# Making part of the gathered far keys by one-hot products in the second attention's main loop

## The chip, the cores and the metric

The kernel runs on one core of one Trainium2 chip, as one program. The metric is the time of one execution on the device in microseconds (us). Each kernel is run several times and the median counts.

## The reference

The model has two layers on 2048 tokens of 128 features: an attention and a mixture of experts each, all with a layer norm in front and a residual behind. The change lies in the second layer's attention. It picks keys for each query:

```
c_kv = x @ W_dkv
s_i = relu(einsum('bthd,bsd->bths', x @ idx_wq, x @ idx_wk))   # 4 index heads
I = einsum('bths,h->bts', s_i, idx_w)
I = where(local, inf, I)       # the last 64 keys are always taken
I = where(causal, -inf, I)
_, idx = top_k(I, 96)          # so 32 far keys by index score
key_c, value = (c_kv @ W_uk)[idx], (c_kv @ W_uv)[idx]
key_r = pope((x @ W_kr)[idx], angles_k)    # angle by the key's rank
attn = softmax((q_c . key_c + q_r . key_r) * scale)   # 8 heads
out = (attn . value) @ W_out
```

The kernel multiplies W_uk into the queries and W_uv into the output, so that a key is one row of 64 numbers: 32 of c_kv, 32 of the softplus of x @ W_kr, which is then turned by an angle that depends on its rank. The 32 far keys of a query are 32 such rows, and they differ from query to query.

## The kernel before, in words

The tokens are cut into 16 tiles of 128 queries. `projections1` computes the key rows, the queries and the index products' operands, keeps the rows in `rows` [128, 16, 64] and writes them to a table in DRAM, `key_table`. It also ranks the first three tiles and issues the first 40 gathers.

`selected_attention` is the main loop. All its engines walk through one list of work, written out ahead by `selected_schedule`, in **slots**: 8 slots for each tile, one group of 16 queries in each. Each engine takes its own items of the list in that order and waits by semaphores; nothing is reordered when it runs. A slot holds, where they exist:

- ("score", t, g), TensorE: the masked scores of a group into one of three banks: mask (L1874), the 256 nearest keys (L1876), the far keys (L1882).
- ("q", ...), ("far", ...), ("p", ...), TensorE, emptied by ScalarE: transposes of queries (L1848), of far keys (L1852) and of probabilities (L1855) through two banks `a1_turn` that all of them share in turn. ("y", ...) is the output product (L1858), which VectorE adds to x (L1821).
- ("max", ...), ("exp", ...), ("den", ...), ("norm", ...): the softmax, on VectorE and ScalarE.
- ("ctx", t, c), TensorE: the weighted sum of half a tile (L1894, L1899); it is the last reader of the far keys.
- ("idx", ...), ("relu", ...), ("sum", ...), ("rank", ...): index scores of a tile some slots ahead on TensorE (L1933, L1934), ScalarE and VectorE (L1786), and its ranking on VectorE in 13 steps (max, max_index, match_replace four times over: L1720, L1723, L1726). `index_schedule` spreads them evenly by their widths over slots 0 to 106. They end with the transpose of the 32 places into `placeT` (L1733).
- ("keys", t, half), VectorE: the rotation of 16 gathered columns of far keys in place (L1092 to L1098), two slots ahead of their use, that of tile t's first half at slot 8t and of its second at slot 8t + 4. ("spin", ...) is the same for queries.

POOL has only the gathers (L1622): one indirect DMA fetches one column, that is one far key row for each of 128 partitions. A tile has 32 columns (tile 0: 16). Partition 32b + r of column i holds the key of rank r of query 32b + i. They go into a ring of four buffers `far`, so tile t waits for the context sums of tile t - 4:

```
if t >= RING:
    pool.wait_ge(ctx_full, 2 * (t - RING + 1))
```

SP's queue issues the few other DMAs of the loop: a copy of half of qT for each tile, the second mask, and the angles for the queries' rotation.

Of the kernel before, what the change touches and what calls it, by code (L numbers as in the profile page):

```python
# [1100 lines left out]
def projections1(nc, dram, x, ident, keep):  # L1101
    with ExitStack() as ctx:
# [22 lines left out]
        flipped = sb("first_flipped", [P, FAR], U32)  # L1125
        work = norm_work(sb, "2")
# [13 lines left out]
        loads = [(keep["idx_w"], "idx_w"), (keep["cap0"], "cap0"), (keep["cap"], "cap"), (cos_k, "cos_k"), (sin_k, "sin_k"),  # L1140
# [40 lines left out]
        with nc.Block() as block:  # L1181
# [85 lines left out]
            def _(dve):  # L1267
# [38 lines left out]
                def first_rank(t):  # L1306
# [4 lines left out]
                    last, cap = (values, keep["cap0"]) if t == 0 else (values[:, index_width(t) - P:], keep["cap"])  # L1311
# [125 lines left out]
PLACES = 6  # L1437
# [34 lines left out]
def selected_schedule(slot, ranking):  # L1472
# [13 lines left out]
    work += [("far", t, j % NG // 2)] if j % 2 == 0 and 0 <= t < NT else []  # L1486
    work += group("max", j - 2) + group("exp", j - 3)
# [9 lines left out]
    work += [("ahead", part, 0)] if 0 <= part < 3 + AHEAD else []  # L1497
    ahead = j + 2
# [30 lines left out]
def gather_list():  # L1529

    return [(t, i) for t in range(NT) for i in range(gathers(t))]


def landed(t, half):

    return 256 * (t // RING + (0 if t % RING == 0 and half else 1))
# [12 lines left out]
def selected_attention(nc, dram, x, ident, keep):  # L1549


    with ExitStack() as ctx:
# [15 lines left out]
        probsT = sb("a1_probsT", [P, 3, NG, P], F32)  # L1568
        biggest = sb("biggest", [P, NG], F32)
# [9 lines left out]
        mask_in, y_added, q_copied = (sem(n) for n in ("mask_in", "y_added", "q_copied"))  # L1579
        sums_done = lambda n: n - (n + NIDX - 1) // NIDX  # L1580
# [4 lines left out]
        TURNS = ("q", "far", "p", "y")  # L1585
# [4 lines left out]
        rotations = [w for w in schedule if w[0] in ("keys", "spin")]  # L1590

        with nc.Block() as block:
            @block.sync
            def _(sp):
# [5 lines left out]

                for t in range(NT):
# [25 lines left out]
            def _(act):  # L1627
                def empty_turn(kind, t, i):
# [32 lines left out]
                for kind, t, i in schedule:  # L1661
                    if kind in TURNS and kind != "y":
# [42 lines left out]
            def _(dve):  # L1705
                own = Order(dve, own_sem)

                def rank(t, i):
# [4 lines left out]
                    if i == 0:  # L1713
                        dve.wait_ge(summed, sums_done(idx_no["idx", t, len(index_chunks(t)) * NIDX - 1]))

                        cols, cap = (slice(0, w), keep["cap0"]) if t == 0 else (slice(w - P, w), keep["cap"])
# [110 lines left out]
            def _(pe):  # L1827
                def fill_turn(kind, t, i):
# [5 lines left out]
                    elif before:  # L1834
                        pe.wait_ge(turn_free, free_no[before])
# [451 lines left out]
```

## Time and profile before

| | us |
|---|---|
| median of 3 runs | 2267.05 |
| fastest and slowest of them | 2263.79, 2666.24 |
| the profiled execution | 2263.79 |
| its span, first to last instruction | 2263.8 |

The page covers the whole program. The first attention takes its first two thirds, the first experts follow, and the second attention begins near 1500 us; its main loop runs from about 1580 to 2217 us, and the last experts end the program. An engine's busy share over the whole span says little about the loop, so the loop is read by stretches. In the stretches a mean granted clock (PEclk) of 1.00 is 2.4 GHz and 0.50 is 1.2 GHz. Slots are found in the timeline by VectorE's rotations of far keys: the first is tile 0's, and each further tile has two.

### The profile page before, as it was taken

Reading aid. Unit: us, or ns where it says so; the run is one execution under the profiler, and the core shown is the slowest. Engines: PE = TensorE matmul, PEld = TensorE weight load, DVE = VectorE, ACT = ScalarE, POOL = GpSimd, SP = SyncE. Lnnn points to the kernel's source line nnn. Section 1 sums busy time; section 2 is a strip of 40 time slices with the busy share of each in tenths; the row PEclk is TensorE's granted clock in tenths of the full one; section 3 lists DMA queues with packets and bytes.
Section 4 is the critical chain, followed back from the end, with each engine's and each line's share of the span. In section 5 each row is a group of like instructions: output and inputs, shape, how many; then the busy total and the mean of one; then the engine's idle time right before and its main releaser. Section 6 shows DMA issues by size and latency. Waiting matters only on the chain. (4 is left out here: it accounts for less than half of the span.)

```text
span 2263.8 us, 56900 instructions
## 1 busy us (share of the span) xinstructions
PE 2100.6 (93%) x22674; PEld 1263.2 (56%) x22674; DVE 1789.1 (79%) x3457; ACT 1732.0 (77%) x3507; POOL 1828.5 (81%) x1239
## 2 busy tenths in 40 slices
PE   5899999999999999999999989986999899988878
PEld 1466666666666666666666646652454444444444
DVE  7788888888888888888888658978868986887214
ACT  5798898998989988988989945657566775775543
POOL 4899999999999999999999945627777777777720
PEclk9999999999999999999999989978579996999878
DMA  4000000000000000000000000111211111111101
GB/s 153 1 2 2 2 2 2 2 2 2 2 2 2 2 2 2 2 2 2 2 2 2 2 15 23 39 39 27 52 38 32 38 33 38 31 38 36 39 10 37
DMA packets 44688, 43.19 MB, mean 19 GB/s; under 512 B 21312, under 2 KB 33424, under 8 KB 44176
## 3 DMA queue, kind: packets, MB, share of 16 engines
q1 hardware_dynamic: 28560, 23.35, 3.6%
q0 software_dynamic: 15872, 16.28, 3.1%
q8 instruction: 178, 2.92, 0.5%
q14 instruction: 78, 0.64, 0.1%
HBM read 33.83 MB, written 1.57 MB: 16 GB/s over the span
## 5 line engine op out<-in xcount | busy, mean ns | idle before, releaser
L380 POOL TENSOR_TENSOR probs_lo<-probs,probs_hi 128x1024 f16<-128x1024 f32 x512 | 1076.7, 2129 | 43.0 <-ACT probs L430 42.6
L494 DVE TENSOR_REDUCE part_max<-aux 128x1 f32<-128x512 f32 x1024 | 677.9, 687 | 91.0 <-PE aux L568 86.7
L429 ACT ACTIVATE probs_hi<-scores 128x512 f16<-128x512 f32 x1024 | 630.2, 615 | 134.6 <-PE scores L601 117.3
L430 ACT ACTIVATE probs<-scores 128x512 f32<-128x512 f32 x1024 | 636.6, 622 | 0.0
L1622 POOL DMA_INDIRECT far<-key_table,placeT x456 | 451.9, 991 | 142.9 <-issue 138.7
L617 PE MATMUL acc<-v,probs_hi 128*128 128x65 f16 x4096 | 451.1, 193 | 2.3 <-POOL probs_lo L380 2.3
L619 PE MATMUL acc<-v,probs_hi 128*128 128x64 f16 x4096 | 452.3, 195 | 0.0
L621 PE MATMUL acc<-v,probs_lo 128*128 128x65 f16 x4096 | 450.6, 192 | 0.0
L617 PEld LDWEIGHTS acc<-v,probs_hi 128*128 128x128 f16 x4096 | 382.5, 96 | 82.6 <-POOL probs_lo L380 2.5
L619 PEld LDWEIGHTS acc<-v,probs_hi 128*128 128x128 f16 x4096 | 380.0, 97 | 75.5
L568 PE MATMUL aux<-k_a,q_a 128*128 128x512 f16 x1024 | 392.1, 383 | 5.2 <-DVE roped L480 2.1
L600 PE MATMUL scores<-q_a,k_a 128*128 128x512 f16 x1024 | 388.9, 380 | 6.6 <-ACT probs L430 6.5
L601 PE MATMUL scores<-q_b,k_b 65*128 65x512 f16 x1024 | 390.0, 381 | 0.0
L621 PEld LDWEIGHTS acc<-v,probs_lo 128*128 128x128 f16 x4096 | 381.6, 99 | 0.0
L601 PEld LDWEIGHTS scores<-q_b,k_b 65*128 65x128 f16 x1024 | 100.1, 98 | 112.6 <-issue 0.5
L568 PEld LDWEIGHTS aux<-k_a,q_a 128*128 128x128 f16 x1024 | 100.1, 98 | 83.1 <-DVE part_max L494 13.8
L600 PEld LDWEIGHTS scores<-q_a,k_a 128*128 128x128 f16 x1024 | 100.4, 98 | 81.5 <-ACT probs L430 26.0
L851 POOL TENSOR_TENSOR e_hid_lo<-e_hid,e_hid_hi 128x512 f16<-128x512 f32 x64 | 74.3, 1162 | 61.3 <-ACT e_hid_hi L803 61.3
L472 DVE TENSOR_TENSOR rope_term<-aux,cos 128x512 f32<-128x512 f32 x128 | 88.5, 691 | 26.4 <-PE aux L551 23.4
L1786 DVE SCALAR_TENSOR_TENSOR space<-space,idx_w 128x512 f32<-128x512 f32 (+4 forms) x111 | 72.8, 656 | 44.0 <-ACT space L1675 40.7
L1876 PE MATMUL a_score<-near_keys,qT 64*128 64x256 f32 x256 | 103.6, 489 | 0.0
L480 DVE TENSOR_TENSOR roped<-aux,rope_term 128x512 f32<-128x512 f32 x128 | 88.6, 692 | 17.6 <-DVE aux L475 1.0
(329 smaller groups left out, 3935.5 us busy)
## 6 DMA issues: line engine op xcount, KB each, us to landing
far<-key_table,placeT POOLq DMA_INDIRECT x496, 2.4
qT<-qT SPq DMA_DIRECT2D x16, 256.0 KB, 2.9
e_w<-in_e_w SPq DMA_DIRECT2D x48, 64.0 KB, 1.9
x<-in_x SPq DMA_DIRECT2D x4, 256.0 KB, 3.9
cos<-in_cos SPq DMA_DIRECT2D x1, 1024.0 KB, 6.8
sin<-in_sin SPq DMA_DIRECT2D x1, 1024.0 KB, 8.9
e_w<-in_e_w SPq DMA_DIRECT2D x2, 512.0 KB, 3.9
out<-x SPq DMA_DIRECT2D x4, 256.0 KB, 2.7
```

Source lines behind the costliest of these rows:

```text
L380: pool.tensor_tensor(probs_lo[:, slot], probs[:, wide], probs_hi[:, slot], ALU.subtract).then_inc(low_ready, 1)
L429: act.activation(probs_hi[:, slot, i], bank, ACT.Exp, scale=float(DH0) ** -0.5)
L430: act.activation(probs[:, wide, i], bank, ACT.Exp, scale=float(DH0) ** -0.5).then_inc(probs_ready, 1)
L494: dve.tensor_reduce(part_max[g % 2][:, n % QT, n // QT:n // QT + 1], bank, AX.X, ALU.max).then_inc(aux_free, 1)
L568: ins = pe.matmul(bank, qa[g % QRING][:, t * P:(t + 1) * P], ka[h % 2][:, c * CH:(c + 1) * CH], start=True, stop=True)
L600: pe.matmul(out, ka[h % 2][:, keys], qa[g % QRING][:], start=True, stop=False)
L601: pe.matmul(out, kb[h % 2][:, keys], qb[g % QRING][:], start=False, stop=True).then_inc(scores_ready, 1)
L617: pe.matmul(out, probs_hi[:, n % SLOTS, i, queries], high, start=(kt == 0 and t == 0), stop=False, skip_group_check=True)
L619: pe.matmul(out[:, 0:DH0], probs_hi[:, n % SLOTS, i, queries], low, start=False, stop=False, skip_group_check=True)
L621: ins = pe.matmul(out, probs_lo[:, n % SLOTS, i, queries], high, start=False, stop=(kt == KT0 - 1), skip_group_check=True)
L1622: pool.indirect_dma_start(far[m][:, i, :], None, keep["table"], bass.IndirectOffsetOnAxis(ap=placeT[t % PLACES][:, i:i + 1], axis=0)).then ...
L1876: pe.matmul(b[:, 0:WIN], qT[t % 2][0:KW, 0, 4 * g:4 * g + 4].rearrange("k i a h -> k (i a h)"), near[:, t * P:t * P + WIN], start=False, s ...
```

## The change

In tiles 3 to 9 (`MADE`) POOL gathers only columns 0 to 15. Columns 16 to 31 are made by TensorE from `rows`, which is in SBUF: the product of a one-hot matrix (which key each partition wants) and the rows of all keys up to the tile's end.

- After the ranking of such a tile VectorE also casts the places to half precision (`place16`). SP stores the part that belongs to columns 16 to 31 to DRAM (four DMAs) and loads all 2048 places of it back to all 128 partitions (one DMA, 512 KB, `placeB`), in `spread_places`.
- ("hot", t, k), k = 0 to 3, VectorE: for each of the t + 1 key tiles one comparison of 512 places with the partition's key number, which gives the one-hot tiles of four columns. They are written into `qi`, over index queries that are no longer needed: a ring of 4 tiles for t = 3, of 8 after it. A place in the ring is written again when TensorE has read it.
- ("make", t, k), one slot later, TensorE: (t + 1) x 2 x 4 products of 128x128 with 64 columns into a turn bank; the rows are split into a high and a low half-precision part (`split`), so that their sum is close to the float value. ScalarE copies the bank (256 columns) into `far`.
- `rows` are split once: a cast on ScalarE, a subtraction on VectorE. `split` and `placeB` lie over the queries of tiles 0 to 2, which are no longer needed then.
- VectorE's rotation of the second half of such a tile waits for the copy instead of the gathers. `placeT` has 5 buffers in place of 6, and `cap0` moves to `projections1`.

The diff, without the changes that only pass names or allocate:

```diff
-PLACES = 6
+PLACES = 5
+MADE = range(3, 10)
+MADE_AT = 3 - NG
+PER = 4
+MAKES = FAR // 2 // PER
+SPLIT = MADE[-1] + 1
+SPLIT_AFTER = ("exp", 1, 0)
...
     work += [("far", t, j % NG // 2)] if j % 2 == 0 and 0 <= t < NT else []
+    made = j - 1 - MADE_AT
+    work += [("make", made // NG, made % NG)] if made // NG in MADE and made % NG < MAKES else []
     work += group("max", j - 2) + group("exp", j - 3)
...
+    t = (j - MADE_AT) // NG
+    work += [("hot", t, (j - MADE_AT) % NG)] if t in MADE and (j - MADE_AT) % NG < MAKES else []
     ahead = j + 2
...
-    return [(t, i) for t in range(NT) for i in range(gathers(t))]
+    return [(t, i) for t in range(NT) for i in range(gathers(t) - (PER * MAKES if t in MADE else 0))]
...
+        hots = [(t, k, kt) for t in MADE for k in range(MAKES) for kt in range(t + 1)]
+        hot_no = {h: n + 1 for n, h in enumerate(hots)}
+        inner_no = {h: n + 1 for n, h in enumerate(h for h in hots if h[2] < h[0])}
+
+        def ring_of(t):
+
+            return NIDX * (2 if t > MADE[0] else 1)
+
+        def hot_tile(t, k, kt):
+
+            e = (k * (t + 1) + kt) % ring_of(t)
+            return qi[:, e % NIDX, (e // NIDX) * CH:(e // NIDX + 1) * CH]
+
+        def wait_used(eng, t, k, kt):
+
+            if kt < t:
+                eng.wait_ge(hot_used, inner_no[t, k, kt])
+            else:
+                eng.wait_ge(turn_full, turn_no["make", t, k])
...
+                def spread_places(t):
+                    n = MADE.index(t)
+                    sp.wait_ge(place16_ready, n + 1)
+                    for b in range(P // 32):
+                        sp.dma_start(dram["places"][n].rearrange("(i b r) -> b i r", i=PER * MAKES, b=P // 32)[b],
+                                     place16[n % PLACES][32 * b + 32 - PER * MAKES:32 * b + 32, :]).then_inc(place_out, 16)
+                    sp.wait_ge(place_out, (n + 1) * (P // 32) * 16)
+                    if n == 0:
+                        sp.wait_ge(turn_free, free_no["q", 2, 3])
+                    else:
+                        sp.wait_ge(hot_ready, hot_no[MADE[n - 1], MAKES - 1, MADE[n - 1]])
+                    sp.dma_start(placeB, dram["places"][n:n + 1].broadcast_to([P, PER * MAKES * P])).then_inc(placeB_in, 16)
...
                     sp.dma_start(qT[t % 2][KW:2 * KW, 1], qT[t % 2][0:KW, 1]).then_inc(q_copied, 16)
+                    if t + 1 in MADE:
+                        spread_places(t + 1)
...
+                    elif kind == "make":
+                        if i == 0:
+                            if t >= RING:
+                                act.wait_ge(ctx_full, 2 * (t - RING + 1))
+                        ins = act.activation(far[t % RING][:, FAR + PER * (i - MAKES):FAR + PER * (i + 1 - MAKES), :],
+                                             src[:, 0:PER * KW].rearrange("p (i k) -> p i k", i=PER), ACT.Copy)
...
+                def hot(t, k):
+
+                    if k == 0:
+                        dve.wait_ge(placeB_in, 16 * (MADE.index(t) + 1))
+                        dve.wait_ge(idx_full, idx_no["idx", ring_of(t) - 1, len(index_chunks(ring_of(t) - 1)) * NIDX - 1])
+                    for kt in range(t + 1):
+                        o = hots.index((t, k, kt)) - hots.index((t, 0, 0))
+                        if o >= ring_of(t):
+                            wait_used(dve, *hots[hots.index((t, k, kt)) - ring_of(t)])
+                        elif k == 0 and kt == 0 and t > MADE[0]:
+                            wait_used(dve, *hots[hots.index((t, 0, 0)) - 1])
+                        dve.tensor_scalar(hot_tile(t, k, kt), placeB[:, k * CH:(k + 1) * CH], key_id[:, kt:kt + 1], None,
+                                          ALU.is_equal).then_inc(hot_ready, 1)
...
                     elif kind == "keys":
                         m = t % RING
-                        dve.wait_ge(far_in[m][i], landed(t, i))
+                        if t in MADE and i:
+                            dve.wait_ge(turn_free, free_no["make", t, MAKES - 1])
+                        else:
+                            dve.wait_ge(far_in[m][i], landed(t, i))
...
+                def make_keys(b, t, k):
+
+                    if k == 0:
+                        pe.wait_ge(split_ready, 1)
+                    for kt in range(t + 1):
+                        pe.wait_ge(hot_ready, hot_no[t, k, kt])
+                        for part in range(2):
+                            for i in range(PER):
+                                ins = pe.matmul(b[:, i * KW:(i + 1) * KW], hot_tile(t, k, kt)[:, i * P:(i + 1) * P],
+                                                split[:, kt, part * KW:(part + 1) * KW], start=(kt + part + i == 0),
+                                                stop=(kt == t and part == 1), skip_group_check=True)
+                        if kt < t:
+                            ins.then_inc(hot_used, 1)
+                    return ins
```

The work that is there already keeps its slots. Of tile t the comparisons stand at the ends of slots 8t - 3 to 8t, the products in slots 8t - 2 to 8t + 1, behind the slot's scores and far transposes. Two places show it, both in slots 70 and 71, where tile 9's keys are made and tile 8 is scored.

TensorE before, from the scores of slot 70 on:

```order
L1874 MATMUL a_score<-mask,unit 128x384
L1876 MATMUL a_score<-near_keys,qT 128x256
L1882 MATMUL a_score<-farT,qT 32x128 x4
L1852 MATMUL a_turn<-ident,far 128x128 x4
L1848 MATMUL a_turn<-ident,queries 64x128 x4
L1933 MATMUL a_idx<-ki_hi,qi 128x512
L1934 MATMUL a_idx<-ki_lo,qi 128x512
```

And with the change:

```order
L1983 MATMUL a_score<-mask,unit 128x384
L1985 MATMUL a_score<-near_keys,qT 128x256
L1991 MATMUL a_score<-farT,qT 32x128 x4
L1961 MATMUL a_turn<-ident,far 128x128 x4
L1927 MATMUL a_turn<-queries,qi 128x64 x80
L1957 MATMUL a_turn<-ident,queries 64x128 x4
L2042 MATMUL a_idx<-ki_hi,qi 128x512
L2043 MATMUL a_idx<-ki_lo,qi 128x512
```

L1927 is the new row (`queries` is `split`, which lies over them): 80 products stand between a slot's far transposes and everything behind them.

VectorE before, from a group's maximum in slot 69 on (a_den is the softmax's sum, place and a_top the ranking):

```order
L1816 TENSOR_REDUCE biggest<-a_score 128x1
L1824 RECIPROCAL a_den<-a_den 128x1
L1786 SCALAR_TENSOR_TENSOR space<-space,idx_w 128x512
L1723 MAX_INDEX place<-a_top,space 128x8
L1816 TENSOR_REDUCE biggest<-a_score 128x1
L1824 RECIPROCAL a_den<-a_den 128x1
L1726 MATCH_REPLACE space<-a_top,space 128x1600
L1816 TENSOR_REDUCE biggest<-a_score 128x1
```

And with the change:

```order
L1907 TENSOR_REDUCE biggest<-a_score 128x1
L1915 RECIPROCAL a_den<-a_den 128x1
L1874 SCALAR_TENSOR_TENSOR space<-space,idx_w 128x512
L1785 MAX_INDEX place<-a_top,space 128x8
L1847 TENSOR_SCALAR qi<-queries,key_id 128x512 x10
L1907 TENSOR_REDUCE biggest<-a_score 128x1
L1915 RECIPROCAL a_den<-a_den 128x1
L1788 MATCH_REPLACE space<-a_top,space 128x1600
L1847 TENSOR_SCALAR qi<-queries,key_id 128x512 x10
L1907 TENSOR_REDUCE biggest<-a_score 128x1
```

L1847 is the new row: ten comparisons stand in front of the next group's maximum (`queries` is `placeB` here).

## Rows read from the trace of the kernel before

**Rows 1.** The page: busy us and share of the span; POOL's busy tenths in 40 slices.
```profile
PE 2100.6 (93%) x22674; PEld 1263.2 (56%) x22674; DVE 1789.1 (79%) x3457; ACT 1732.0 (77%) x3507; POOL 1828.5 (81%) x1239
...
POOL 4899999999999999999999945627777777777720
```

**Rows 2.** The gathers of L1622: ns min/median/max, first and last start; idle before them; landing.
```profile
L1622 POOL DMA_INDIRECT far<-key_table,placeT x456: 938/944/1962, 1579.6 to 2169.2; - x152
...
  issue: 138.7, 455
...
DMA to landing us min/median/max: 2.3/2.4/4.4
```

**Rows 3.** VectorE's waits for landings: us, times, longest; timeline of first and last (start, us).
```profile
DVE far_turned L1092 <- DMA far<-key_table,placeT: 56.5, 5, 13.3
...
2089.65 0.69 DVE L1092 TENSOR_TENSOR far_turned<-far,cos_far 128x512 f32<-128x512 f32 x1 [6.29 <-DMA far<-key_table,placeT]
...
2171.53 0.69 DVE L1092 TENSOR_TENSOR far_turned<-far,cos_far 128x512 f32<-128x512 f32 x1 [13.15 <-DMA far<-key_table,placeT]
```

**Rows 4.** Timeline of VectorE: the first rotation of tile 13.
```profile
2072.34 0.68 DVE L1092 TENSOR_TENSOR far_turned<-far,cos_far 128x512 f32<-128x512 f32 x1
```

**Rows 5.** Busy us by stretch (PE, PEld, DVE, ACT, POOL), granted clock, DMA share, GB/s.
```profile
1682.00:1935.00 253.00, 232.65 (x1728) 124.81 (x1726) 204.77 (x370) 175.74 (x407) 193.57 (x196) 0.90 0.16 36
...
2072.00:2172.00 100.00, 77.95 (x599) 44.21 (x598) 36.98 (x117) 53.19 (x121) 74.65 (x78) 0.84 0.16 36
...
1750.00:1800.00 50.00, 44.94 (x369) 24.10 (x369) 46.63 (x86) 39.15 (x88) 38.12 (x40) 1.00 0.18 41
```

**Rows 6.** The two longest waits of TensorE, then of VectorE, from 1682 to 1935 us.
```profile
PE a_ctx L1894 <- ACT a_probsT L1645: 12.4, 7, 2.0
PE a_score L1874 <- ACT a_probs L1687: 4.8, 9, 1.0
...
DVE space L1786 <- ACT space L1675: 21.2, 17, 2.8
DVE x L1821 <- PE a_turn L1858: 20.3, 4, 9.8
```

**Rows 7.** Timeline of TensorE: the second context sum of tile 6.
```profile
1888.32 1.92 PE L1899 MATMUL a_ctx<-a_probsT,far 128*32 128x32 f32 x32
```

**Rows 8.** Timeline of TensorE in the first attention: first of 24 products, and what follows them.
```profile
699.95 0.19 PE L617 MATMUL acc<-v,probs_hi 128*128 128x65 f16 x1
...
700.69 0.38 PE L568 MATMUL aux<-k_a,q_a 128*128 128x512 f16 x1
```

**Rows 9.** VectorE's groups by form: busy us, mean ns.
```profile
L1786 DVE SCALAR_TENSOR_TENSOR space<-space,idx_w 128x512 f32<-128x512 f32 x72 | 53.4, 742 | 29.6 <-ACT space L1675 28.1 <-DVE space L1786 0.5
L1098 DVE TENSOR_TENSOR far<-far_turned,far_swapped 128x512 f32<-128x512 f32 x31 | 21.5, 692 | 1.1
L1349 DVE TENSOR_SCALAR softplus_u<-softplus_e 128x1024 f32<-128x1024 f32 x4 | 2.8, 688 | 1.4 <-ACT softplus_e L1258 1.4
...
L1349 DVE TENSOR_SCALAR softplus_key_u<-space 128x256 f32<-128x256 f32 x2 | 0.6, 294 | 7.6 <-ACT space L1258 7.6
```

**Rows 10.** ScalarE's groups from 1682 to 1935 us.
```profile
L1675 ACT ACTIVATE space<-a_idx 128x320 f32<-128x320 f32 x4 | 1.6, 430 | 0.0
```

**Rows 11.** DMA issues: count, size, median us to landing.
```profile
qT<-qT SPq DMA_DIRECT2D x16, 256.0 KB, 2.9
...
mask<-in_mask SPq DMA_DIRECT2D x1, 768.0 KB, 4.3
```

**Rows 12.** Busy us and granted clock of short stretches, columns as in rows 5.
```profile
1660.00:1670.00 10.00, 10.00 (x39) 5.72 (x39) 2.31 (x7) 3.87 (x11) 7.56 (x9) 0.50 0.11 27
...
1900.00:1910.00 10.00, 10.00 (x43) 5.01 (x43) 8.83 (x13) 5.34 (x12) 7.82 (x8) 0.50 0.12 27
1960.00:1970.00 10.00, 8.20 (x82) 4.96 (x82) 8.69 (x11) 6.15 (x16) 7.87 (x8) 1.00 0.12 28
...
699.00:702.00 3.00, 3.00 (x37) 1.72 (x35) 2.50 (x4) 3.00 (x7) 2.32 (x2) 1.00 0.00 0
```

More of the change, by code:

```diff
@@ L1139, in projections1 @@
             keep[n] for n in ("rows", "queries", "near_keys", "nout", "qi", "ki_hi", "ki_lo"))
-        loads = [(keep["idx_w"], "idx_w"), (keep["cap0"], "cap0"), (keep["cap"], "cap"), (cos_k, "cos_k"), (sin_k, "sin_k"),
+        loads = [(keep["idx_w"], "idx_w"), (cap0, "cap0"), (keep["cap"], "cap"), (cos_k, "cos_k"), (sin_k, "sin_k"),
                  (keep["mask"], "mask_first"), (keep["unit"], "unit"), (keep["cos_far"], "cos_far"),
@@ L1310, in first_rank @@
                     dve.wait_ge(first_summed, (NIDX - 1) * (t + 1))
-                    last, cap = (values, keep["cap0"]) if t == 0 else (values[:, index_width(t) - P:], keep["cap"])
+                    last, cap = (values, cap0) if t == 0 else (values[:, index_width(t) - P:], keep["cap"])
                     own.link(dve.tensor_tensor(last, last, cap[:], ALU.min))
@@ L1529, in gather_list @@
 def gather_list():
-    return [(t, i) for t in range(NT) for i in range(gathers(t))]
+    return [(t, i) for t in range(NT) for i in range(gathers(t) - (PER * MAKES if t in MADE else 0))]
 def landed(t, half):
-    return 256 * (t // RING + (0 if t % RING == 0 and half else 1))
+    return 256 * sum(half == 0 or s > 0 and s not in MADE for s in range(t % RING, t + 1, RING))
 def keys_no(t, half):
@@ L1568, in selected_attention @@
         probsT = sb("a1_probsT", [P, 3, NG, P], F32)
+        place16 = [sb(f"place16_{i}", [P, FAR], F16) for i in range(PLACES)]
+        key_id = sb("key_id", [P, SPLIT], F32)
+        split = QN[:, 0].rearrange("p h c -> p (h c)").bitcast(F16)[:, 0:SPLIT * 2 * KW].rearrange(
+            "p (t k) -> p t k", t=SPLIT)
+        placeB = QN[:, 1:3].rearrange("p t h c -> p (t h c)").bitcast(F16)[:, 0:PER * MAKES * P]
         biggest = sb("biggest", [P, NG], F32)
@@ L1661, in _ @@
                 for kind, t, i in schedule:
+                    if (kind, t, i) == SPLIT_AFTER:
+                        act.wait_ge(turn_full, turn_no["q", 0, 3])
+                        act.activation(split[:, :, 0:KW], rows[:, 0:SPLIT, :], ACT.Copy).then_inc(high_ready, 1)
                     if kind in TURNS and kind != "y":
@@ L1714, in rank @@
                         dve.wait_ge(summed, sums_done(idx_no["idx", t, len(index_chunks(t)) * NIDX - 1]))
-                        cols, cap = (slice(0, w), keep["cap0"]) if t == 0 else (slice(w - P, w), keep["cap"])
-                        own.mark(dve.tensor_tensor(values[:, cols], values[:, cols], cap[:], ALU.min))
+                        last = values[:, w - P:w]
+                        own.mark(dve.tensor_tensor(last, last, keep["cap"][:], ALU.min))
                     elif i % 3 == 1:
@@ L1732, in rank @@
                                 dve.wait_ge(far_in[before % RING][half], landed(before, half))
+                        if t in MADE:
+                            n = MADE.index(t)
+                            if n >= PLACES:
+                                dve.wait_ge(place_out, (n - PLACES + 1) * (P // 32) * 16)
+                            dve.tensor_copy(place16[n % PLACES][:], place[:]).then_inc(place16_ready, 1)
                         dve.transpose(placeT[t % PLACES][:], place[:]).then_inc(place_ready, 1)
@@ L1835, in fill_turn @@
                         pe.wait_ge(turn_free, free_no[before])
+                    if kind == "make":
+                        make_keys(b, t, i).then_inc(turn_full, 1)
+                        return
                     if kind == "q" and i == 0:
```

16 lines of the change are left out of this document (14 added, 2 removed).

## The prediction

> **What bounds the kernel now.** I read the page first, then the busy times by stretch, the waits, and the timeline where the stage changes pace. The stage at stake is the second attention's main loop, from about 1580 us to 2217 us. The page shows every engine busy there and POOL fullest in all the slices [rows 1], which suggests that POOL's gathers set the pace. The next views say otherwise for most of the stage. POOL issues its 456 gathers from 1579.6 to 2169.2 us with only its own issue gaps between them [rows 2]: 589.6 / 455 = 1.296 us each, 41.5 us for a tile of 32. Yet VectorE, whose rotation of the far keys is the first reader of what they bring, waits for a landing in five places only, 56.5 us in all, the first at 2089.65 us [rows 3]. Until the first rotation of tile 13 at 2072.34 us [rows 4] the readers are slower than POOL, and use up the lead that it got before the loop.
>
> What they run into shows in the stretches [rows 5]. From 1682 to 1935 us (slots 21 to 72, where the change puts its work) TensorE is busy 232.65 of 253 us, VectorE 204.77, ScalarE 175.74. TensorE's idle 20.3 us are mostly waits for ScalarE [rows 6]; VectorE's idle 48 us are mostly waits for ScalarE's share of the index scores and for TensorE's output product [rows 6]. So TensorE paces, with VectorE close: in its fullest 50 us VectorE is busy 46.63 us, 93% [rows 5]. Only from 2072 to 2172 us is the loop POOL's: VectorE 36.98 busy, TensorE 77.95 [rows 5].
>
> **What the change takes off POOL.** 7 tiles x 16 gathers = 112, x 1.296 = 145 us of POOL. Little of it arrives. POOL has four far buffers, so tile 10, the first full one again, cannot start before the second context sum of tile 6, which ends at 1888.32 + 1.92 = 1890.2 us [rows 7]. Six tiles then take 192 x 1.296 = 248.8 us, and 2.4 us to land [rows 2]. With the readers undelayed, the last keys land at 2141.4 us, where they are now waited for until 2171.5 us. From there to the end are 2263.8 - 2171.5 = 92.3 us that the change does not touch. **The floor** is thus 2141.4 + 92.3 = 2234 us, plus whatever the added work delays tile 6.
>
> What comes next once the five waits go is TensorE. The 100 us from 2072 to 2172 hold 77.95 us of it at a mean granted clock of 0.84 [rows 5], so nearly a third of them at 1.2 GHz; I let half of that return to 2.4 GHz (-8), and leave 6 us for its waits on ScalarE: 76 us. The end comes **24 us** earlier. (Bounds: 18, if TensorE's time stays and 4 us of wait; 30, if the clock is 2.4 GHz throughout.)
>
> **What it adds to TensorE.** For tile t, four fills of (t+1) x 8 products of 128x128 half-precision weights with 64 columns. The tiles' t+1 add up to 49: 49 x 32 = 1568 products. Their nearest kin are the first attention's 128x65 and 128x64: 24 of them start between 699.95 and 700.69 us, 31 ns apart (not the 190 ns printed for one, which overlap) [rows 8]. 1568 x 0.031 = 48.6 us at 2.4 GHz. Clock 0.90 [rows 5] means a fifth of the stretch at 1.2 GHz; doubling that fifth of them gives 58 us.
>
> **What it adds to VectorE.** 196 comparisons, 128x512, half precision in and out, with one [P,1] operand. No row has this form. Nearest by bytes is the 128x256 float tensor_scalar, 294 ns [rows 9]. The [P,1] operand adds 50 ns: 742 for the 128x512 scalar_tensor_tensor that has one, 692 for the tensor_tensor [rows 9]. Instructions without a wait between them start 0.07 us before the last one's printed end. So 0.344 - 0.07 = 0.28 us each, 55 us; with seven small casts (0.2 each) and one 640-column subtraction (0.8) it is 57 us. Bounds: as many elements at the float form's slope, (688 - 294) / 768 = 0.51 ns [rows 9], give 0.40 us each, 79 us; one element a cycle, 0.67 each, 131 us.
>
> The Trainium skill, VectorE: DVE Perf Modes, "The perf-mode tier table", has tensor_scalar at four elements a cycle for 16-bit data in SBUF, which is what the byte count gives; no row here shows it. By its table of N=2048 (128 cycles plus about 158) the instruction would take 298 ns and the 196 some 9 us less than above.
>
> **Together.** Between slots 21 and 72 VectorE comes to 204.8 + 57 = 262 us; at its best fill, 93%, that needs 281 us: +28. TensorE comes to 232.7 + 58 = 291; if its 20 us of idle stay, 311: +58. The low end asks for the clock to rise, the high end that nothing fills. I take **+44**, midway.
>
> **What I cost at nothing.** ScalarE empties 28 more banks of 256 columns, under the 430 ns of a 320-column one [rows 10], 12 us at most, plus one cast: it has 77 us idle in the stretch. Each tile's spreading of places is a half-precision store and a 512 KB load back on SP's queue. The mask's 768 KB land in 4.3 us and small copies in 2.9 [rows 11]: 8 us in series. In the order written out it has the five slots between one tile's last comparison and the next tile's first, over 20 us. Without that cover VectorE would stand 4 us a tile. SP's copy of qT comes five slots later and its angle loads later still.
>
> **Sum.** 2263.8 + 44 - 24 = 2284 us on the profiled execution, which is the fastest of the three runs; the median is 3.3 us above it, so **2287 us**. POOL is no longer last: four fifths of the comparisons (39 of 49) lie before tile 6's sum, which comes 35 us later, so the keys land at 2176 us and are wanted at 2191.5.
>
> **Rivals.**
> - *The clock is lifted and the idle fills (0.20).* From 1660 to 1670 and 1900 to 1910 us the clock is 0.50, with TensorE printed busy 10.00 of 10; from 1960 to 1970 it is 1.00 at busy 8.20 [rows 12]. The first attention's half-precision products of this form run at 1.00 [rows 8, 12]. If the added ones keep it at 2.4 GHz, TensorE needs 232.7 - 25 + 48.6 = 256 us and VectorE 262; +15 in all. The tail then falls by 30: 2249 us, 2252 on the median's scale. Against it: the busy value alone did not hold the clock in two of three rows. The Trainium skill, TensorE: Matmul & The Clock Gate, "What's actually happening", says that low is the default and activity releases it, which would favour this case; by the busy column the trace agrees only in part.
> - *Slower: the two engines take turns (0.15).* The comparisons write into eight tiles that the products read. With 9 and 10 needed per fill (tiles 8 and 9) VectorE cannot finish one set before TensorE has begun the next slot's fill, and in all tiles set k+1 overwrites what fill k reads. TensorE in turn stands before each fill, with scores and index products queued behind. If VectorE waits through the fills, 204.8 + 57 + 58 = 320 us, and with half of its present idle 344: +91 - 24 gives 2331, 2334. It is over 2% once the stretch grows by 69 us. For it: ring and order. Against it: fills are one slot behind, and only two tiles overrun the ring.
> - *Slower: comparisons at one element a cycle (0.07).* 204.8 + 133 = 338 us even without idle, +85: 2325, 2328.
> - *The places come late (0.03).* Seven waits of 4 us or more before a tile's first comparison, up to 30 us: about 2310.
>
> **Chances.** The forecast has 0.55, with its own range 2265 to 2310. About 2% is what a measurement of this kernel can tell from no change: 2222 and 2312 us. Faster than that is below the floor of 2234, and would need the work before tile 6's sum to become quicker: 0.03. Slower: the second rival, the third, and a little of the forecast: 0.22. Within: 0.75. The range of 8 in 10 takes the forecast, the first rival and the lower part of the slow ones: 2240 to 2328.
>
> **What would show it.** Right: no landing wait of VectorE in the last three tiles, or only short ones; POOL idle before tiles 5 to 10; rotation of tile 9 near 1976 us, that of tile 13 near 2116; comparisons about 0.34 us, products 31 ns apart at clock 1.00. Wrong: comparisons at 0.7 us; VectorE waiting in front of the comparisons for products, more than 3 us a fill; the granted clock over 0.97 in tiles 3 to 9; or the five landing waits still there, which would mean that the ring held POOL longer than I count.

## The result, and the profile after

The changed kernel takes **2308.49 us** (median of 4 runs, 2304.84 to 2309.89) against 2265.86 us of the kernel before beside it (4 runs; the median of 2267.05 shown ahead is over 3 of them, and the one of 2666.24, in a slower state, does not enter the ratio): a ratio of **1.0187, interval 1.0171 to 1.0202**, or 42.6 us more. The forecast was 2287, 20 us more. The time is inside the range and the kernel is slower, as forecast, but the cost is twice what the sum gave.

The experiments below came to other chips. On five of them the kernel before took 2754 to 2758 us, on one 2266.6, as for the result. Times are therefore compared only within one job (kernels run together on one chip), or as ratios to the kernel before of the same job.

The page of the changed kernel: span, engines, and POOL's busy tenths in 40 slices.

```profile
span 2302.8 us, 60245 instructions
...
PE 2137.6 (93%) x24242; PEld 1305.3 (57%) x24242; DVE 1843.5 (80%) x3661; ACT 1741.7 (76%) x3536; POOL 1717.7 (75%) x1127
...
POOL 4899999999999999999999836547632334677700
```

Against [rows 1] POOL has lost 111 us and has holes: it now waits for the ring of far buffers. The gathers, what ended the idle time before them, and their landing:

```profile
L1675 POOL DMA_INDIRECT far<-key_table,placeT x344: 940/944/1736, 1577.7 to 2192.4; - x172
...
  PE a_ctx L2008: 171.8, 8
  issue: 103.3, 335
...
DMA to landing us min/median/max: 2.3/2.5/4.8
```

VectorE's rotations of far keys mark the pace. Its timeline in the changed kernel, the first rotations of tiles 8, 9 and 13, and the last one (start, us):

```profile
1936.42 0.69 DVE L1092 TENSOR_TENSOR far_turned<-far,cos_far 128x512 f32<-128x512 f32 x1
...
1988.00 0.71 DVE L1092 TENSOR_TENSOR far_turned<-far,cos_far 128x512 f32<-128x512 f32 x1
...
2129.20 0.67 DVE L1092 TENSOR_TENSOR far_turned<-far,cos_far 128x512 f32<-128x512 f32 x1
...
2206.77 0.67 DVE L1092 TENSOR_TENSOR far_turned<-far,cos_far 128x512 f32<-128x512 f32 x1
```

None of the 31 waits for a landing any more; the five waits of [rows 3] are gone. Tile 9's first rotation, at 1988.00, came at 1932.9 us before; tile 10's follows at 2021.85 (before 1966.7). Tile 13's came at 2072.34 [rows 4], the last at 2171.53 [rows 3]. Read as intervals, the 39 us between the two spans are:

| stretch | before | after | difference |
|---|---|---|---|
| start to tile 2's second rotation | 1679.6 | 1674.6 | -5.0 |
| from there to tile 10's first (slots 21 to 80; all of it by tile 9's first, slot 72) | 287.1 | 347.3 | **+60.2** |
| to tile 13's first | 105.6 | 107.3 | +1.7 |
| to the last rotation (the tail) | 99.2 | 77.6 | **-21.6** |
| to the end | 92.3 | 96.0 | +3.7 |

The stretch of the added work, columns as in [rows 5], from tile 2's second rotation to tile 9's first: the kernel before, then the changed one.

```profile
1679.60:1932.86 253.26, 232.91 (x1726) 124.83 (x1726) 205.03 (x371) 175.91 (x405) 193.78 (x196) 0.89 0.16 36
```

```profile
1674.60:1988.00 313.40, 278.25 (x3241) 170.98 (x3242) 258.10 (x570) 184.62 (x431) 116.41 (x120) 0.91 0.13 32
```

The same without its first 2.4 us, and the tail; under them the added products alone and the comparisons alone in these 311 us:

```profile
1677.00:1988.00 311.00, 276.14 (x3235) 169.92 (x3236) 255.73 (x565) 182.34 (x425) 114.62 (x118) 0.92 0.13 32
2129.20:2206.80 77.60, 68.07 (x506) 39.16 (x506) 36.83 (x117) 47.28 (x108) 49.40 (x50) 0.78 0.16 35
...
1677.00:1988.00 311.00, 56.99 (x1522) 54.11 (x1523) 0.92 0.13 32
...
1677.00:1988.00 311.00, 54.80 (x196) 0.92 0.13 32
```

Between the same two rotations the loop takes 60.1 us more. The products are 57.0 us of TensorE. The rest of its work went from 232.9 to 221.3 us, at a granted clock of 0.91 instead of 0.89. Its idle time went from 20.4 to **35.2 us**. 57.0 - 11.7 + 14.8 = 60.1 us. (The 253 us of [rows 5] end 2 us behind tile 9's rotation, so 311 - 253 = 58 would be 2 us too little.) What TensorE waited for in these 311 us, and then VectorE's waits in front of the comparisons (us, times, longest):

```profile
PE a_turn L1927 <- DVE qi L1847: 15.0, 6, 4.4
PE a_ctx L2003 <- ACT a_probsT L1704: 9.6, 7, 1.6
PE a_score L1983 <- ACT a_probs L1749: 5.4, 14, 0.9
...
DVE qi L1847 <- PE a_turn L1927: 13.7, 3, 5.6
```

The waits for ScalarE are nearly what they were [rows 6]; the first line is new, and it is as long as the growth of the idle time. Where these six waits lie says what they are. Four of them, 2.42, 4.13, 3.35 and 4.39 us, stand before the third fill of tiles 3, 5, 7 and 9 and make 14.3 of the 15.0 us. Each time VectorE has its rotation of the queries just in front of those comparisons, eight instructions of 4.2 us in all, which comes once in two tiles. In tile 9, the last of the eight, the comparisons, and then TensorE:

```profile
1973.10 0.69 DVE L1098 TENSOR_TENSOR queries<-far_turned,far_swapped 128x512 f32<-128x512 f32 x1
1973.71 2.85 DVE L1847 TENSOR_SCALAR qi<-queries,key_id 128x512 f16<-128x512 f16 x10
...
1974.20 4.35 PE L1927 MATMUL a_turn<-queries,qi 128*128 128x64 f16 x80 [4.39 <-DVE qi L1847]
```

So these waits come from the order of VectorE's own list, not from the ring: in tiles 3, 5 and 7 it never waits for a place in the ring. A kernel with the comparisons in front of the rotation was not run. The comparisons themselves, by form (ns min/median/max), with the place where tile 9's last set waits for products:

```profile
L1847 DVE TENSOR_SCALAR qi<-queries,key_id x196: 311/347/547, 1682.5 to 1987.7; 128x512 f16<-128x512 f16 x196
...
1987.47 0.62 DVE L1847 TENSOR_SCALAR qi<-queries,key_id 128x512 f16<-128x512 f16 x2 [5.60 <-PE a_turn L1927]
```

### The profile page after: what moved, and what is told of

Its sections match the earlier page's. It is cut to its first block and busy times, and to the rows that moved or that the text cites. A ratio compares the mean times of both kernels' runs of the same rounds, so it can differ in the third digit from the quotient of the medians.

```text
span 2302.8 us, 60245 instructions
## 1 busy us (share of the span) xinstructions
PE 2137.6 (93%) x24242; PEld 1305.3 (57%) x24242; DVE 1843.5 (80%) x3661; ACT 1741.7 (76%) x3536; POOL 1717.7 (75%) x1127
## 5 line engine op out<-in xcount | busy, mean ns | idle before, releaser
L1675 POOL DMA_INDIRECT far<-key_table,placeT x344 | 340.7, 990 | 280.3 <-PE a_ctx L2008 171.8
L475 DVE TENSOR_TENSOR aux<-aux,sin 128x512 f32<-128x512 f32 x128 | 89.5, 699 | 13.2 <-PE aux L551 0.2
```

The lines of the kernel that those rows point to most:

```text
L475: dve.tensor_tensor(bank, bank, keep["sin"][:, cols], ALU.mult).then_inc(rope_turned, 1)
L1675: pool.indirect_dma_start(far[m][:, i, :], None, keep["table"], bass.IndirectOffsetOnAxis(ap=placeT[t % PLACES][:, i:i + 1], axis=0)).then ...
```

## The experiments

**1. Why the kernel before takes 2757 us on some chips.** The kernel before, unchanged, for a trace of it there.

> The kernel before itself, for a trace of it where it takes about 2757 us; the trace at hand is of a run of 2264 us. Where its 490 us more are: theory F, TensorE's instruction supply starves while GpSimd issues gathers, so TensorE has nothing to do in each burst of gathers (456 of them in this part): the stretch ahead of the first gather is within 1 us of the other trace, and of the 490 us more nearly all lie between the first and the last gather, while each instruction's own duration is unchanged; no 16 KB packet of the instruction queue falls inside a long burst. Theory G, the chip is slower in general: every stretch is longer by the same share. If it runs at 2265 us, it only repeats what is known.

It took 2753.23 us, in one execution; the seven others of that job have a median of 2758.37. Its first 1500 us hold 1436.87 us of TensorE's work, the other trace's 1437.61: nothing is slower there. The difference begins with the gathers. The stretch by columns as in [rows 5], first of this run, then the same microseconds of the trace of 2264 us:

```profile
1607.00:1637.00 30.00, 18.26 (x78) 7.80 (x77) 12.61 (x29) 12.39 (x21) 22.64 (x24) 0.67 0.15 33
1637.00:1697.00 60.00, 0.03 (x1) 0.00 (x0) 4.09 (x9) 0.00 (x0) 45.36 (x49) 0.50 0.15 26
...
1709.00:1768.00 59.00, 55.40 (x312) 25.94 (x311) 48.62 (x104) 38.42 (x86) 0.00 (x0) 0.65 0.09 26
```

```profile
1637.00:1697.00 60.00, 57.62 (x376) 31.32 (x375) 42.26 (x86) 39.32 (x89) 45.98 (x47) 0.76 0.16 37
```

POOL issues 72 gathers in a row from 1607.3 to 1697.5 us. TensorE works for the first third, then stands for the rest of the burst and 11 us more. So do the others: in the 60 us of the second line ScalarE is busy for 0.00 us and VectorE for 4.09. TensorE's timeline, and the next gather after the burst, which waits for the ring:

```profile
1636.42 0.60 PE L1934 MATMUL a_idx<-ki_lo,qi 64*128 64x512 f16 x1
1708.35 0.61 PE L1933 MATMUL a_idx<-ki_hi,qi 128*128 128x512 f16 x1 [71.33 <-ACT space L1675]
...
1768.12 0.94 POOL L1622 DMA_INDIRECT far<-key_table,placeT  x1 [70.61 <-PE a_ctx L1899]
```

TensorE's wait of 71.33 us ends with ScalarE. What held ScalarE and VectorE the profile does not name; it prints "remote", as it never does in the two traces of the result. Their longest such waits in this trace (us, times, longest):

```profile
DVE biggest L1816 <- remote: 204.4, 22, 29.2
ACT a_probsT L1645 <- remote: 189.4, 13, 26.2
ACT farT L1641 <- remote: 160.1, 14, 68.4
```

The last one's 68.4 us lie in this burst and the 7 us behind it. So POOL runs a burst while the three other engines stop in its later part, and then waits for them. Which engine stops first, or whether something holds them all, is not shown. The DMA queues between 1610 and 1700 us, of the trace of 2264 us and then of this run:

```profile
q0 software_dynamic: 2239, 2.30, 11.3%
q1 hardware_dynamic: 1457, 1.57, 6.2%
q8 instruction: 4, 0.07, 0.3%
```

```profile
q0 software_dynamic: 2272, 2.33, 13.8%
q1 hardware_dynamic: 80, 0.26, 1.1%
q14 instruction: 1, 0.01, 0.0%
```

As many gather packets pass in both, and no packet of the large instruction queue (q8) in the second. Theory G, a chip slower throughout, falls. Theory F's place holds, and its size for the most part: 426 of the 488 us more lie between the first of all gathers (1521.1 and 1522.0 us) and the last (2169.2 and 2595.9). The other 61 lie behind it, where VectorE's last rotation of far keys comes 58 us after the last gather instead of 2. The cause that theory F names is not shown. It speaks of TensorE alone, and the others stop too; and the next 16 KB packet comes only after TensorE has gone on, so the empty queue may be a consequence.

**2. One part at a time.** Four variants in three jobs, all on chips of the 2757 us kind. Edits to the changed kernel:

```diff
 gathers alone:          no "hot" and "make" items, no place16, no spreading of places
 comparisons alone:      no "make" items
 products alone:         no "hot" items, no place16, no spreading of places; operand qi[:, kt % NIDX, 0:CH] for hot_tile(t, k, kt)
 both, uncoupled:
-                            wait_used(dve, *hots[hots.index((t, k, kt)) - ring_of(t)])
+                            dve.wait_ge(hot_ready, hot_no[t, k, kt] - ring_of(t))
-                        pe.wait_ge(hot_ready, hot_no[t, k, kt])
-                                ins = pe.matmul(b[:, i * KW:(i + 1) * KW], hot_tile(t, k, kt)[:, i * P:(i + 1) * P],
+                                ins = pe.matmul(b[:, i * KW:(i + 1) * KW], (ki_hi[:, kt % NCH * CH:(kt % NCH + 1) * CH])[:, i * P:(i + 1) * P],
```

All four leave the made key columns without their keys. Expected of the gathers alone:

> GpSimd's 112 gathers of tiles 3 to 9 are gone as in the change, but neither the comparisons nor the products are made (those key columns hold zeros or old keys). This leaves the saving alone. On a chip with the kernel before at 2266 us, all theories: the landing waits behind tile 13 go (-24 us), the rest stays, 2236 to 2243 us. If the gathers' absence is also worth something between slots 21 and 72, it comes out under 2236.

Of the comparisons alone, and of the products alone:

> As the first, with the spreading of places and the 196 comparisons on VectorE, but no products that read them. Theory A (TensorE paces, and of what the change cost beyond its products 15 to 29 us are waits of VectorE and TensorE for each other): VectorE has 48 us of idle to put 54 us of work into, and it costs 15 to 30 us over the first: 2255 to 2270. Theory B (the engines' work is in series, slot by slot, so added work on either shows in full): 50 to 57 us over it, 2290 to 2297.

> As the first, with the 1568 products on TensorE and ScalarE's copies into far, but no comparisons: the products read old index queries. Theory A: TensorE paces, so 57 us of products less what a higher clock gives back show nearly in full, 35 to 50 us over the first: 2275 to 2290. Theory B: 57 us, 2295.

Of both uncoupled, and of the changed kernel beside it:

> Both added works are done in full number and at their places, but the products take their moving operand from another array instead of the comparisons' result, and the comparisons do not wait for the products to free a buffer: TensorE and VectorE no longer wait for each other on account of the change. Theory A (the idle of TensorE grew by what it waits for comparisons): 15 to 29 us under the changed kernel, so 2279 to 2293 us where that is at 2308. Theory B (VectorE and TensorE do their added work in turns, so either engine's share is paid in full): over 2300 only if the turns come from other waits. Theory C (the new waits are a symptom; TensorE's idle time is the loop's own and the products' 57 us are simply added): within 5 us of the changed kernel, 2303 to 2313 us.

> The changed kernel itself once more, beside the variants on the same chip, since the first four variants ran on a chip on which the kernel before took 2755 us and cannot be set against the 2308 us measured for the change. Where the kernel before takes about 2266 us: 2305 to 2310 us. If the chip is again the one on which the kernel before takes 2755 us: the variants with both added works and no mutual waits took 80 us over the one with neither there; theory A (15 to 29 us of the cost are waits of TensorE and VectorE for each other) then gives this one 15 to 29 us over r4_both_uncoupled, theory C (the waits are a symptom, they only show idle time that was there before) within 5 us of it.

| | first job | second job | third job |
|---|---|---|---|
| kernel before | 2755.37 | 2757.41 | 2754.38 |
| gathers alone | 2617.53 | 2624.27 | |
| comparisons alone | 2620.26 | | |
| products alone | 2703.30 | | |
| both, uncoupled | 2697.24 | 2690.91 | 2705.84 |
| the change | | 2711.07 | |

Three things follow. **The change is faster here**: 0.9832 (0.9791 to 0.9873). Taking 112 gathers away gives 133 us, 1.19 us for each, nearly its whole issue time; the added work costs 87. **Theory B falls**: the comparisons alone cost 3 us, where it had 50 to 57. Theory A fares no better there, with 15 to 30. The products alone cost 86 us, more than the 35 to 57 of both theories and more than their own time of 58. So here what VectorE was given lies beside TensorE's work. **The mutual waits** cost 20 us by the second job (2705 to 2716 against 2686 to 2696 us), as theory A had it; the changed kernel's trace of that job has 17.6 us of VectorE's waits for products and 12.1 us of TensorE's for comparisons. The third job's run of the same variant has a ratio of 0.9809 (0.9769 to 0.9850), too near to the change's to tell them apart. On a chip of the result's kind no variant of this experiment was run.

**3. All gathers back, the rest of the change kept.** ScalarE copies the made keys to a place aside.

```diff
-    return [(t, i) for t in range(NT) for i in range(gathers(t) - (PER * MAKES if t in MADE else 0))]
+    return [(t, i) for t in range(NT) for i in range(gathers(t))]
```

> The whole change with GpSimd loading all 32 columns of every tile as before. Where the kernel before takes 2266 us: theory D (the change delays the loop so much that no landing is waited for any more, with or without the 112 gathers) within 6 us of the changed kernel, 2303 to 2314 us; theory E (each removed gather is worth its time) some 20 us over it, about 2330 us, with landing waits behind tile 13. Where it takes 2757 us: 2855 to 2890 us, as before.

2884.44 us in one job, 173 more than the change beside it, and 2878.93 in another (ratio 1.0442, 1.0394 to 1.0490): 1.55 us for each gather. By this comparison each removed gather is worth more than its issue time on these chips, where bursts of gathers stop the other engines.

For the result's kind of chip theory D against E was not run, but the changed kernel's own trace there speaks for D. POOL's first gathers of tiles 9 and 10:

```profile
1888.03 0.94 POOL L1675 DMA_INDIRECT far<-key_table,placeT  x1 [27.94 <-PE a_ctx L2008]
...
1932.66 0.94 POOL L1675 DMA_INDIRECT far<-key_table,placeT  x1 [23.65 <-PE a_ctx L2008]
```

Before tile 10 POOL stood for 23.65 us. The 16 gathers taken from tile 9 would fill 16 x 1.296 = 20.7 of them, and tile 8's would fit in front of tile 9 in the same way. By this estimate tile 10, and all that POOL does after it, would have come when they did with every gather in place.

**4. Fewer tiles.** `MADE = range(3, 5)` and `range(3, 8)` for `range(3, 10)`.

> The change for two tiles only (3 and 4) instead of seven: 16 instead of 56 comparison and product steps' worth of added work, and GpSimd loads all columns of tiles 5 to 9. GpSimd's lead over the loop is limited by the ring of far-key buffers, so what 32 removed gathers save (41 us of issue) is about what the ring lets it use. Where the kernel before takes about 2266 us: the added work costs 60 us x 2/7 = 17 us (theory A: 12 to 17, since the first tiles of the change show few mutual waits), the landing waits at the tail give back 21 to 24 us if 41 us of lead are enough, 2253 to 2262 us; if the lead is lost again in tiles 5 to 12, there is nothing to set against the cost, 2278 to 2283 us. Where the kernel before takes about 2757 us (the other condition in which the first eight runs were made, where the variants without the 112 gathers were 133 us faster, 1.19 us for each, and the added work cost 87 us): 32 gathers give 38 us, the added work costs 25 us, 2740 to 2748 us.

> The change for tiles 3 to 7 only: in these the comparisons of one step number at most the ring's 8, while in tiles 8 and 9 they number 9 and 10 and the last ones wait for products of the step before (13.7 us of VectorE's waits in the changed kernel's trace). The added work is 30/49 of the change's. Where the kernel before takes 2266 us: theory A (mutual waits, which are mostly in tiles 6 to 9): work 57.2 x 30/49 = 35 us less the 14 us that the rest of the loop gained, some 5 us of waits, and a tail gain of 22 us, 2266 to 2275 us; if the cost is simply in proportion, 60 x 30/49 - 22 = +15 us, 2280 us. Where it takes 2757 us: 80 gathers fewer at 1.19 us give 95 us, the added work 80 x 30/49 = 49 us, the waits up to 5 us: 2711 to 2720 us, no worse than the whole change (2711 us).

Two tiles: 2736.42 us, ratio 0.9937 (0.9916 to 0.9957), and 0.9924 (0.9898 to 0.9949) when repeated; a little better than the 2740 to 2748 expected. Five tiles: 2732.29 us, 0.9903 (0.9879 to 0.9928), 12 us worse than expected. So 2, 5 and 7 tiles give 19, 26 and 46 us; the gain is not in proportion to the gathers, and why the middle tiles give less was not found. Whether two tiles are faster than the kernel before where that takes 2266 us was not measured: both runs came to the other kind of chip.

**5. The gathers spaced.** The changed kernel, with writes of zeros to a scratch area on POOL after every n-th gather.

```diff
+                    if n % 4 == 3:
+                        for k in range(n // 4 * 3, (n // 4 + 1) * 3):
+                            if k:
+                                pool.wait_ge(idled, k)
+                            pool.memset(idle[:], 0.0).then_inc(idled, 1)
```

> The changed kernel with one thing added: in the second attention GpSimd writes zeros to a scratch area six times (about 5 us) after every eighth gather, so its gathers come in bursts of 10 us instead of 20 to 70. In the condition in which the kernel before takes 2757 us TensorE stands still in the later part of a burst (16 gathers: from 13 us after the burst's start to 4 us after its end; 72 gathers: for 71 us). Theory H, a burst must last over some 13 us before it stops TensorE: the stops go, and what bounds is GpSimd's own time, 344 gathers at 1.25 us and 43 pauses of 5 us from 1590 on, last landing near 2235 us and then 100 us: 2330 to 2400 us. Theory I, TensorE is held for a part of each gather's time whatever the spacing: 2700 to 2760 us. If the kernel before takes 2266 us: 2325 to 2345 us, since GpSimd becomes late for the last tiles.

> As the one before with the same share of pause, three writes of zeros (about 2.5 us) after every fourth gather. Theory H as there: bursts of 5 us stop nothing if a pause of 2.5 us ends a burst, 2330 to 2400 us; if the pause is too short to end one (TensorE went on 1 to 12 us after the last gather of a burst), then as without pauses or worse, over 2700 us, while the one with 5 us of pause is faster. Theory I: 2700 to 2760 us for both.

Six writes after every eighth gather: 2529.43 us, ratio 0.9175 (0.9140 to 0.9211). Three after every fourth, as in the diff: **2447.89 us, 0.8880** (0.8859 to 0.8901). On this chip the kernel before takes 2756.44. The second one gives POOL 258 writes, 218 us of work, and is 263 us faster than the change (2711.07, in another job of this kind of chip). The first 167 us of the second one's loop, columns as in [rows 5]:

```profile
1605.00:1772.00 167.00, 148.15 (x984) 75.68 (x984) 126.82 (x276) 98.75 (x215) 140.83 (x151) 0.73 0.17 39
```

TensorE is busy 89% of it beside POOL's gathers, where in experiment 1 it was busy for 0.03 of 60 us. Theory I, with 2700 to 2760 us, falls. Theory H is right in kind, but both times lie above its 2330 to 2400 us, and its 13 us limit does not hold: bursts of 10 us (the first kernel) cost 81 us more than bursts of 5.

> One write of zeros (0.85 us, 1.0 with its wait) after every second gather in the changed kernel. Three writes after every fourth gave 2448 us, with no stop of TensorE over 5 us but 82 us of VectorE's waits for landings, since GpSimd itself was late. Theory H2, what counts is that gathers do not follow one another for more than a few us: no long stops here either, GpSimd needs 344 x 1.25 + 172 x 1.0 = 602 us from 1600 on and lands its last keys near 2200 to 2220 us: 2330 to 2370 us. Theory J, what counts is the share of the time that GpSimd spends in gathers (4 of 6 us there, 2.5 of 3.5 here, all of it in the changed kernel): between the two, 2500 to 2560 us.

> One write of zeros after every fourth gather. Theory H2: bursts of 5 us, as in the kernel that took 2448 us, with a pause of 1 us: no long stops if 1 us is enough to end a burst, and then GpSimd's own 344 x 1.25 + 86 x 1.0 = 516 us no longer bind, 2310 to 2350 us. Theory J: the share of gathers is 5 of 6 us, 2580 to 2650 us. If this one is far slower than the one with a write after every second gather, the pause of 1 us works only behind short bursts.

These two came to a chip where the kernel before takes 2266.61 us: **2350.37 us**, ratio 1.0384 (1.0361 to 1.0406), and 2318.29 us, 1.0230 (1.0210 to 1.0251). So theory H2 against J stays untested; they test the tail of the prediction, on a chip of the result's kind. With a pause after every second gather the loop keeps its pace up to tile 8, though POOL is busier: its first rotation is at 1935.91 us, in the changed kernel 1936.42. Tile 13's is at 2135.42, 6.2 us late, with no wait for a landing before it. Then POOL falls behind. VectorE's waits, and the first and the last of its rotations of far keys that wait:

```profile
DVE far_turned L1092 <- DMA far<-key_table,placeT: 72.4, 5, 18.4
...
2149.68 0.69 DVE L1092 TENSOR_TENSOR far_turned<-far,cos_far 128x512 f32<-128x512 f32 x1 [3.26 <-DMA far<-key_table,placeT]
...
2253.66 0.69 DVE L1092 TENSOR_TENSOR far_turned<-far,cos_far 128x512 f32<-128x512 f32 x1 [18.37 <-DMA far<-key_table,placeT]
```

Five landing waits are back, 26.0 us apart, which is 16 gathers and 8 pauses. The last rotation comes 46.9 us later than in the changed kernel, the end of the span 44.0. The variant with a pause after every fourth gather has a single landing wait, of 5.9 us, and its last rotation is still 20.0 us late: at tile 13 it is 14.1 us (2143.26 against 2129.20), 3.0 of them from before the loop. So POOL's time counts most at the tail. But with a busier POOL 6 and 11 us were also lost ahead of it, where nobody waited for a landing, and why was not found.

## Why the prediction was wrong

- **The step that failed is the +44 for slots 21 to 72, "midway"** between a low end that fills idle time (+28) and a high end at which nothing fills (+58). The measured growth is 60 us between the same two rotations: the high end. The prices of the added work were right, the choice between the ends was not. TensorE's own sum, 232.7 + 58 = 291 us, is already 38 over 253, so +44 left it 6 us of idle time where it had 20. It had 35. The waits for ScalarE stayed, 18.1 of the former 20.3 us; I read them as chains inside a slot that further products do not shorten, which no run shows. And 15 us came on top, which end with a comparison, 14.3 of them behind VectorE's rotation of the queries. That the total comes so near to the high end's 58 is in part luck: these 15 us were not in it, nor were the 11.7 us by which the rest of TensorE's work shrank.
- **By parts**, the profiled execution is 39.0 us longer and the sum had 20: +60.2 to tile 10 instead of +44; -17.9 from tile 13's first rotation to the end (-21.6 and +3.7) instead of -24; +1.7 between the two, and -5.0 before the added work begins, both costed at nothing. The -5.0 was not foreseen and is luck.
- **The price of the products** was 58 us, measured 58.5 us over all 1568 (57.0 of them in the stretch). **The comparisons** were put at 0.344 us by a nearest row and a [P,1] operand's 50 ns; the trace has 0.347, 54.8 us in all. The Trainium skill, VectorE: DVE Perf Modes, "The perf-mode tier table", has 693 ns for 2048 elements; an estimate from it for 512 is 293 ns, not the 298 of my prediction. The measurement decides, and it is 18% over that.
- **The tail**: -24 forecast for the end, -21.6 measured up to the last rotation and -17.9 to the end, just under the lower bound of 18. All five landing waits went, TensorE took over, busy 68.07 of 77.6 us at a clock of 0.78. I had half of the slow time return to 2.4 GHz; none did. TensorE's busy time fell by 10 us for another reason: 506 of its instructions fall in the stretch instead of 599 [rows 5], and 441 instead of 360 behind the last rotation. So the term is near, but not for the reason given. (Its upper bound of 30 comes out at 32 by its own terms.) The variant with a pause after every second gather shows the landing waits from the other side.
- **The -24 and the +44 are not two separate terms.** A loop that is 60 us late wants its last keys at 2206.8 us. The kernel before, with all 456 gathers, had them at 2171.5. The sum itself had them wanted at 2191.5. So the delay alone can take the landing waits away, and by the estimate in experiment 3 the 112 gathers taken away bought next to nothing here. No run on this kind of chip tests it.
- **The ring**: POOL waits 171.8 us for context sums. The floor let tile 10 wait for tile 6's sum and all after it run through; POOL stood once more, 9.1 us before tile 11, and the last gather started at 2192.4 us, so the keys landed near 2195 and not at 2176. They were wanted at 2206.8, so it cost nothing.
- **The rival in which the engines take turns** was right about the place: VectorE waits in tiles 8 and 9, where 9 and 10 comparisons meet a ring of eight, 2.9 to 5.6 us a time. Two of the three waits meet the prediction's sign of being wrong, "more than 3 us a fill". It was wrong about the size, 13.7 us instead of a whole stretch, and TensorE's waits have another source, VectorE's rotation of the queries. A little of it belonged in the forecast: its waits were argued to be small and then counted as zero.
- That the 15 us of TensorE's waits are the cause of the missing 16 us is read from the trace by their equal size. The one direct comparison (20 us, second job) was made where bursts of gathers stop the engines, and its repeat did not separate. So it points that way and is not shown.
- **The clock-lifted rival**: 0.91 in the stretch, 0.89 before; the products did not hold it at 1.00. The rest of TensorE's work shrank by 11.7 us, presumably in part by this clock, which hid as much of the failed step.

## What to carry to other kernels

Do not take idle time of the pacing engine that hangs on short waits for a neighbour as room for more work: here 18 of its 20 us stayed. Add new work to it in full, and look what stands in front of the new producer in its own list. A transfer that is hidden is worth its time only where it is waited for, here in the last 100 us. And a delay and a saving that act on the same wait cannot be added up: the delay may take the wait away by itself. Before taking such a sum to another chip, look whether a long burst of indirect DMAs stops the other engines there, since the same edit was 1.9% slower on one kind and 1.7% faster on the other.

## What was not expected of the hardware

The same kernel took 2266.6 us on one chip and 2754 to 2758 us on five others. Up to the first gathers the traces agree within 1 us in 1500. From there TensorE, ScalarE and VectorE stand in the later part of a long burst of indirect DMAs, TensorE up to 71 us, while POOL's issues keep their 1.25 us. Spacing the gathers (4, then 2.7 us of zeros) made it 11.2% faster than the kernel before on such a chip; a lighter spacing (4, then 0.9 us) cost 10 us over the change on a chip of the other kind, where no such stops are seen. What makes a chip behave so, and whether the instruction queue is its cause, was not found.
